# Alternating the two feed-forward products block by block, earlier gathers for the experts, and a semaphore clearing without its own barrier

## The reference, cut to what matters

```python
def _L0_ffn_ref(x, Wr, br, Wi, bi, Wg, bg, Wo, bo, gamma, beta):      # 8 experts, the best 2 of each token
    h = gelu(xf @ Wi_e + bi_e) * sigmoid(xf @ Wg_e + bg_e)
    r = xf + (h @ Wo_e + bo_e)                                        # then normalised, scaled and shifted
def _L1_ffn_ref(x, ln_gamma, ln_beta, fc1_q, fc1_scales, fc1_bias, fc2_q, fc2_scales, fc2_bias):
    h = (x - mu) * rsqrt(var + EPS) * ln_gamma + ln_beta
    y = silu(h.reshape(-1, H) @ dequant(fc1_q, fc1_scales) + fc1_bias)   # 256 -> 1024
    z = y @ dequant(fc2_q, fc2_scales) + fc2_bias                        # 1024 -> 256
    return x + 0.5 * z
x = _layernorm(x + _L0_attn_ref(...))       # a test-time-training layer
x = _layernorm(x + _L0_xattn_ref(...))
x = _layernorm(x + _L0_ffn_ref(...))        # mixture of experts
x = _layernorm(x + _L1_attn_ref(...))       # causal self-attention, 16 heads
x = _layernorm(x + _L1_xattn_ref(...))      # cross-attention over 1601 keys
x = _layernorm(x + _L1_ffn_ref(...))
```

## Time and profile before

| | |
|---|---|
| Median of 3 timed runs | 1908.94 us (1908.84 to 1918.33) |
| The profiled execution's own time | 1901.39 us |
| Its span | 1899.6 us, 33937 instructions |
| PE busy | 1710.2 us, 90% |
| DVE, ACT, POOL busy | 1366.7, 1041.8, 672.3 us |
| Expert stage, first to last PE product | about 405 to 756 us |
| Self-attention ends, cross-attention stage begins | 1054.3, 1059.9 us |
| Last stage | 1772.7 us to the end |

### The profile page before, as it was taken

One profiled execution on the slowest core, in us unless ns is written; L12 is line 12 of the kernel. 1 busy time (PEld: TensorE's weight loads), 2 busy tenths in 40 slices (PEclk: granted clock), 3 DMA queues, 4 the chain that ended last, 5 costly groups with the idle time before them and its releaser, 6 DMA issues. The chain is left out here.

```text
span 1899.6 us, 33937 instructions
## 1 busy us (share of the span) xinstructions
PE 1710.2 (90%) x13150; PEld 937.8 (49%) x13150; DVE 1366.7 (72%) x2346; ACT 1041.8 (55%) x1743; POOL 672.3 (35%) x754
## 2 busy tenths in 40 slices
PE   8999899989999997889999788599999999999786
PEld 4788577758888886423333555122222222223354
DVE  1534688756666666767775578989999999995663
ACT  1221555535555554336667243178888888886442
POOL 0555877124444442323320234313322121102452
PEclk9999999989999999969999899589999999999998
DMA  5134899866777673621110476321201011100001
GB/s 196 35 118 150 301 318 319 293 256 262 296 276 284 260 281 137 183 83 32 33 30 10 144 198 208 88 62 41 81 19 36 18 27 28 24 14 1 26 12 33
DMA packets 114083, 247.58 MB, mean 130 GB/s; under 512 B 28234, under 2 KB 83054, under 8 KB 110320
## 3 DMA queue, kind: packets, MB, share of 16 engines
q1 hardware_dynamic: 87636, 208.21, 31.6%
q0 software_dynamic: 24176, 35.12, 6.9%
q10 hardware_dynamic: 2112, 2.10, 0.3%
HBM read 183.39 MB, written 61.38 MB: 129 GB/s over the span
## 5 line engine op out<-in xcount | busy, mean ns | idle before, releaser
L2114 DVE TENSOR_REDUCE Eh_maxima<-Eh_max 128x2 f32<-128x802 f32 x512 | 474.7, 987 | 20.4 <-PE Eh_max L1993 15.3
L2102 ACT ACTIVATE Eh_probs<-Eh_pair 128x1024 f32<-128x1024 f32 (+1 forms) x288 | 287.5, 998 | 112.5 <-PE Eh_pair L2032 112.4
L1993 PE MATMUL Eh_max<-Eh_KS,Eh_QS 49*128 49x401 f16 x1024 | 197.3, 357 | 45.7 <-DVE Eh_maxima L2114 41.7
L1453 PE MATMUL C_y<-C_x_high,C_W 128*128 128x256 f16 (+1 forms) x1536 | 216.3, 254 | 8.9 <-ACT C_gate L1513 7.4
L2055 PE MATMUL Eh_av_ps<-Eh_probs,E_V 128*17 128x512 f32 (+1 forms) x1664 | 222.1, 606 | 0.0
L2114 DVE TENSOR_REDUCE Dh_maxima<-Dh_max 128x2 f32<-128x1024 f32 x128 | 152.1, 1222 | 43.9 <-PE Dh_max L2001 42.0
L1453 PE MATMUL C_y<-C_x_low,C_W 128*128 128x256 f16 (+1 forms) x768 | 181.3, 254 | 0.0
L2102 ACT ACTIVATE Eh_probs<-Eh_single 128x512 f32<-128x512 f32 x272 | 161.7, 595 | 26.8 <-PE Eh_single L2032 26.6
L1993 PEld LDWEIGHTS Eh_max<-Eh_KS,Eh_QS 49*128 49x128 f16 x1024 | 50.3, 94 | 234.2 <-DVE Eh_maxima L2114 199.2
L1831 POOL DMA_DIRECT2D Eh_KS<-E_kd x64 | 37.2, 581 | 352.7 <-PE Eh_pair L2032 347.9
L1453 PEld LDWEIGHTS C_y<-C_x_high,C_W 128*128 128x128 f16 x1536 | 139.5, 98 | 22.6 <-ACT C_gate L1513 9.6
(11 more groups left out here) (433 smaller groups left out, 3549.0 us busy)
## 6 DMA issues: line engine op xcount, KB each, us to landing
C_W<-w_split SPq DMA_DIRECT2D x24, 3072.0 KB, 11.8
w_split<-B_w_parts SPq DMA_DIRECT2D x24, 768.0 KB, 8.4
Eh_KS<-E_kd POOLq DMA_DIRECT2D x64, 150.1 KB, 3.3
C_tail<-in_expert_tail_dram SPq DMA_DIRECT2D x24, 384.0 KB, 8.5
B_places<-in_w_experts_dram SPq DMA_DIRECT2D x10, 768.0 KB, 6.8
A_QT<-in_w_experts_dram SPq DMA_DIRECT2D x8, 768.0 KB, 5.0
w_split<-A_QT SPq DMA_DIRECT2D x8, 768.0 KB, 6.7
early_more<-in_w_experts_dram SPq DMA_DIRECT2D x8, 768.0 KB, 10.0
```

Of the source, the lines that this page charges most:

```text
L1453: last = mm(y_ps[n % Y_BANKS][:, i, 0:w], W[:, u, a, at_w:at_w + P], x[:, s % 2, k, 0:w], start=(q == 0), stop=(q == len(parts) - 1))
L1993: last = self.nc.tensor.matmul(bank[:, a, 0:self.cw], self.QS[r, slot, p, qt * P:(qt + 1) * P], self.KS[r, slot, p, k0:k0 + self.cw], star ...
L2102: self.nc.scalar.activation(dst, src, ACT.Exp, scale=1.0 / SCORE).then_inc(self.exp_done, 1)
L2114: self.nc.vector.tensor_reduce(self.maxima[:, g % 2, :, p * TPB + qt, c], self.max_ps[n % 2][:, :, 0:self.cw], AX_X, ALU.max).then_inc(sel ...
```

## The change

In the expert stage a tile's gather moves from the tail of POOL's loop to its head. The barrier with clearing between self-attention and cross-attention goes; the attention blocks clear, on POOL, those ids that earlier stages have given back. `held.close()` gives the expert stage's semaphores back before the heads of self-attention. The last stage's biases are loaded in the cross-attention stage, where ACT also runs one sigmoid at its end, and the four normalisations of batch 1 move from there into the last stage. In the last stage the second product of block n-2 follows the first product of block n, for all four token tiles at once, each in its own PSUM bank; the hidden halves live in a ring of 8. DVE's and POOL's insertions are placed anew, and the last batch is stored in two parts.

```diff
@@ phase_moe, POOL
             for s in range(TILES):
+                if s + 3 < TILES:
+                    gather(s + 3)
                 if s + 1 < TILES:
                     base(s + 1)
                 for q in range(SIZES[s]):
                     finish(s, q)
                     scatter(s, q)
-                if s + 3 < TILES:
-                    gather(s + 3)
@@ LastStart
+        sp.dma_start(self.b1[:], self.dram["L1_ffn_fc1_bias"]).then_inc(self.small_loaded, 16)
+        sp.dma_start(self.b2[:], self.dram["L1_ffn_fc2_bias"].partition_broadcast(P)).then_inc(self.small_loaded, 16)
+
+    def warm_up(self, act):
+        act.wait_ge(self.scale_loaded, 32)
+        self.nc.scalar.activation(self.warm[:], self.gamma[:], ACT.Sigmoid).then_inc(self.warmed, 1)
...
                 v.tensor_copy(self.HT_parts[:, 0, 0], self.HT[:, 0]).then_inc(self.ht_high, 1)
-                self.normed_again(dve, 1)
@@
+def spent_semaphores(nc):
+
+    free = set(nc.free_semaphores)
+    return runs_of([s for s in nc.released_uncleared_semaphores if s in free])
...
@@ run_heads, and likewise phase_cross1 ahead of start.pool(pool)
+            for first, end in spent:
+                pool.sem_clear(range(first, end))
@@ phase_cross1
                 heads.scalar(act)
+                start.warm_up(act)
@@ phase_last
+    turn_ps = after.turn_ps = [ps(f"turn{h}", [P, S])[:] for h in range(KD)]
+    after.out_ps = [bank.rearrange("p (q d) -> p q d", d=D) for bank in turn_ps]
     y1_ps = [ps(f"y1_{i}", [P, S]) for i in range(2)]
-    y2_ps = [ps(f"y2_{i}", [P, D]) for i in range(2)]
+    y2_ps = [ps(f"y2_{t}", [P, S]) for t in range(TPB)]
@@ phase_last, SP
-            sp.dma_start(b1[:], dram["L1_ffn_fc1_bias"]).then_inc(small_loaded, 16)
-            sp.dma_start(b2[:], dram["L1_ffn_fc2_bias"].partition_broadcast(P)).then_inc(small_loaded, 16)
...
+            for first, end in STORES:
+                sp.wait_ge(norm_out.normed, end)
+                sp.dma_start(out[first * P:end * P, :].rearrange("(t p) d -> p t d", p=P), X[:, first:end, :]).then_inc(stored, 16)
@@ phase_last, PE
+            def narrow(n):
+                c, j = divmod(n, NF)
+                pe.wait_ge(hidden_low, n + 1)
+                for t in range(TPB):
+                    if j == 0 and c >= 1:
+                        pe.wait_ge(sum_ready, (c - 1) * TPB + t + 1)
                     for i, (a, x) in enumerate(((0, 0), (0, 1), (1, 0))):
-                        last = mm(y2_ps[n % 2][:], hidden_parts[:, c % 2, a, j, t * P:(t + 1) * P], w2_parts[:, x, j, :],
+                        last = mm(y2_ps[t][:, 0:D], hidden_parts[:, a, n % RING, t * P:(t + 1) * P], w2_parts[:, x, j, :],
                                   start=(j == 0 and i == 0), stop=(j == NF - 1 and i == 2))
+                    if j == NF - 1 and t < TPB - 1:
+                        last.then_inc(y2_ready, 1)
+                last.then_inc(narrowed, 1)
+
+            widen(0, 0)
             after.attended(pe, B - 1)
+            widen(0, 1)
+            for n in range(2, B * NF):
+                widen(*divmod(n, NF))
+                if n == 2:
+                    pe.wait_ge(after.copied, KD * B)
+                    turn(1)
+                    pe.wait_ge(w_loaded, 16)
+                if n == 5:
+                    pe.wait_ge(copied, 2 * KD)
+                    after.project(pe, B - 1)
+                if n == NF + 2:
+                    pe.wait_ge(after.sum_ready, NT // 2)
+                    turn(2)
+                if n == 2 * NF + 2:
+                    turn(3)
+                if n < B * NF - 1:
+                    narrow(n - 2)
+            for n in range(B * NF - 3, B * NF):
+                narrow(n)
@@ phase_last, POOL
-            for n in range(1, B * NF):
+            for n in range(B * NF):
                 low(n)
+                if n == 2:
+                    start.low(pool, 1)
+                if n == 4:
+                    norm_in.inverse_deviation(pool, 2)
+                if n == NF:
                     after.norm.inverse_deviation(pool, 3)
+                if n == NF + 3:
+                    start.low(pool, 2)
                 if n == NF + 4:
                     norm_in.inverse_deviation(pool, 3)
+                if n == 2 * NF + 3:
+                    start.low(pool, 3)
+                if n in (NF + 4, 2 * NF + 4, 3 * NF + 4):
+                    norm_out.inverse_deviation(pool, n // NF - 1)
...
@@ phase_last, DVE, from block 4 on
+            for n in range(4, B * NF):
+                c, j = divmod(n, NF)
+                step(n)
+                if n == 5:
+                    start.normed_again(dve, 2)
+                if n == 6:
+                    after.add(dve, 3)
+                    after.norm.statistics(dve, 3, after.sum_ready, per=2)
+                if n == NF:
+                    base(1)
+                if c >= 1 and j == 1:
+                    dve.wait_ge(base_ready, c)
+                    for t in range(TPB):
+                        add((c - 1) * TPB + t)
+                if n == NF + 2:
+                    start.again(dve, 3)
+                if c >= 1 and j == 3:
+                    norm_out.statistics(dve, c - 1, sum_ready)
+                if n == NF + 5:
+                    start.normed_again(dve, 3)
+                if n == NF + 6:
+                    base(2)
+                if n == 2 * NF:
+                    base(3)
+                if c >= 1 and j == 5:
+                    dve.wait_ge(norm_out.rstd_ready, c)
+                    normalize((c - 1) * TPB, c * TPB)
+            dve.wait_ge(base_ready, B)
+            for n in range(NT - TPB, NT):
+                add(n)
+                norm_out.statistics_of(dve, n, sum_ready)
@@ build_program
-                    phase_self(nc, own, dram, X, XT, ident, attended, carried, self_loaded)
+                    phase_self(nc, own, held, dram, X, XT, ident, attended, carried, self_loaded)
             routed.close()
-            renew_semaphores(nc)
```

More of the change, by code:

```diff
@@ L2982, in phase_cross1 @@
         start.use_banks(heads.max_ps)
+        spent = spent_semaphores(nc)
         with nc.Block(no_gpsimd_drain=True) as block:
@@ L3022, in phase_cross1 @@
     return start
+RING = 8
+STORES = [(c * TPB, (c + 1) * TPB) for c in range(B - 1)] + [(NT - TPB, NT - 1), (NT - 1, NT)]
 def phase_last(nc, ctx, dram, X, XT, ident, ATT, weight_parts, out, start):
@@ L3095, in _ @@
[L3095 to L3098, removed]
-            after.attended(pe, B - 1)
[L3100 to L3103, removed]
-                for j in range(NF):
-                    widen(c, j)
-                    narrow(c - 1, j // 2, range(NF // 2) if j % 2 == 0 else range(NF // 2, NF))
-                    if (c, j) == (1, 1):
-                        after.project(pe, B - 1)
-                    if (c, j) == (1, 5):
-                        turn(2)
-                    if (c, j) == (2, 5):
-                        turn(3)
@@ L3134, in high @@
             def high(n):
-                c, j = divmod(n, NF)
                 act.wait_ge(hidden_ready, n + 1)
-                if j == 0 and c >= 2:
-                    act.wait_ge(y2_ready, (c - 1) * TPB)
-                nc.scalar.copy(hidden_parts[:, c % 2, 0, j, :], hidden[:, n % 4, :]).then_inc(hidden_high, 1)
+                if n >= RING:
+                    act.wait_ge(narrowed, n - RING + 1)
+                nc.scalar.copy(hidden_parts[:, 0, n % RING, :], hidden[:, n % 4, :]).then_inc(hidden_high, 1)
             def step(n):
@@ L3201, in add, with normalize @@
             def add(n):
-                dve.wait_ge(y2_ready, n + 1)
-                v.scalar_tensor_tensor(X[:, n, :], y2_ps[n % 2][:], 0.5, X[:, n, :], ALU.mult, ALU.add).then_inc(sum_ready, 1)
+                c, t = divmod(n, TPB)
+                if t < TPB - 1:
+                    dve.wait_ge(y2_ready, c * (TPB - 1) + t + 1)
+                else:
+                    dve.wait_ge(narrowed, (c + 1) * NF)
+                v.scalar_tensor_tensor(X[:, n, :], y2_ps[t][:, 0:D], 0.5, X[:, n, :], ALU.mult, ALU.add).then_inc(sum_ready, 1)
+            def normalize(first, end):
+                for n in range(first, end):
+                    norm_out.normalize_of(dve, n)
             dve.wait_ge(small_loaded, 32)
@@ L3207, in _ @@
             step(0)
-            start.again(dve, 2)
+            start.normed_again(dve, 1)
             step(1)
+            after.norm.normalize(dve, 2)
             step(2)
+            norm_in.statistics(dve, 2, after.norm.normed)
+            step(3)
             dve.wait_ge(half_b2, 1)
             base(0)
-            for j in range(3, NF):
-                step(j)
-            for c in range(1, B):
-                for j in range(NF):
-                    step(c * NF + j)
-                    if (c, j) == (1, 0):
-                        start.normed_again(dve, 2)
-                    if (c, j) == (1, 1):
-                        after.add(dve, 3)
```

(20 more changed lines are left out.)

71 lines of the change are left out of this document (26 added, 45 removed).

## The result

The changed kernel takes 1862.54 us (median of 4, 1862.25 to 1863.48) against 1908.89 in the same session: a ratio of 0.9758 (0.9733 to 0.9782). Nine executions of it in two sessions have a median of 1865.5, 32 of the kernel before 1908.8. The forecast, 1874, was 8 to 12 us too high; the time lies at the low end of the range. The profiled execution took 1862.25 us (span 1860.4), 39.2 less in span than the one before, where I had summed 35.1.

A forecast was written before the change was run, and what follows sets the result against it. Expert and feed-forward stages were taken as PE-bound with holes. Gains 16.5 + 5.3 + 0.5 + 1.8 + 10.6 + 0.4 = 35.1 us give 1866.3 from the profiled 1901.39, 1873.8 from the timed 1908.94; forecast 1874, range 1862 to 1886.

The forecast's parts named there:

- Gathers, 16.5: Expert stage: gathers issued one tile sooner remove PE's eight waits, 16.5 of 17.0 us gained, bounds 10 and 17.5.
- rival B: Expert stage: PE waits for weights or biases instead, 1.5 us at each of eight places, 12 in all: 1886 us; chance 0.07.
- Border, 5.3: Between self-attention and cross-attention: dropping the barrier with its clearing gains 5.3 us, POOL's clears being hidden; bounds 3 to 5.6.
- rival D: Attention stages: POOL's clears do not overlap and hold a stage's end, the border's 5.3 us comes back: 1879 us; chance 0.06.
- Clock behind the border, 0.5: Start of cross-attention: PE may keep 2.4 GHz behind the short border, 0.5 us gained, bounds 0 and 3.
- End of cross-attention, 1.8: Without four normalisations on DVE, ACT's copy of the last sums starts 1.8 us sooner, and the next border too; bounds 0 to 1.9.
- Feed-forward stage, 10.6: Last stage: new product order and earlier loads take it from 114.0 to 103.4 us, 10.6 less; bounds 2 and 20.
- rival C: Last stage: PE's many short waits drop it to 1.2 GHz and keep it there, 90 us more: 1964 us; chance 0.03.
- Rival A: Feed-forward stage gains nothing: each block waits 0.35 us for its low half or hidden block, price 10.6: 1884.5 us; chance 0.10.
- Last store, 0.4 less: End of the kernel: the last store is 128 instead of 512 KB, 0.4 us gained, between 0 and 0.8.
- The sum: Whole kernel: all gains added, 35.1 us less than the profiled execution or the timed median.

The follow-up runs named there:

- the seventh: The changed kernel with an empty block at the third border, in which POOL clears the whole range of ids without a drain of POOL: 1866.3 us.
- the ninth run: The changed kernel once more, unchanged: median 1866.12 us, ratio 0.9781 to the kernel before.
- The border experiment: The kernel before with only the third border changed (no barrier, clears on POOL inside the attention stages): 1901.86 us, ratio 0.9965.

## Why the prediction was right, and where not

*Gathers, 16.5:* right, with all eight waits gone; weights and biases did not become late (rival B). Against the mean of the four old profiles it is 19.3, since the profiled one was short in this stage. That is above my bound of 17.5: 1.0 of it is clock, and some 1.3 are not in the list of waits.

*Border, 5.3:* right in size (6.4 to 1.1). The step that named the clearing as what costs was wrong; it was POOL's drain (3.98 us, against 0.78 for the clear). "No row shows a clear by itself" was wrong too: the view of line 3316 has both. That the clears hide (against rival D) held.

*Clock behind the border, 0.5:* the table has 3.4 for that stretch, the repeated change 0.3. That the border has a part in it is not shown: the stage's first 28 us had 3.5 to 6.1 us at the lower clock in the six profiles with the long border, and 0 (twice) to 6.2 in the other eight.

*End of cross-attention, 1.8:* right. With 57.4 us at the lower clock the heads take 573.8 before, 571.9 and 572.0 after (the seventh and the ninth run). The load starts 0.02 us behind the operation ahead of it, and its end and the next sigmoid are 0.01 us apart. The drain of 1.38 us that the Trainium skill, "ScalarE: Activation LUTs" ("What ACT_TABLE_LOAD costs"), adds to the load does not appear here, and the trace decides against it.

*Feed-forward stage, 10.6:* this term was mis-sized; it measured 15.0 (114.0 to 99.0, where I had named 100 to 107 as a sign). Two parts of the step failed. I took a slow start for certain (4.5 us with the filling); in the first trace the clock stayed at 2.4 GHz, and PE's idle times just before had become 0.81 and 1.15 instead of 2.65 and 1.30. These do not settle it: in four of the ten profiles with the changed stage it started at 1.2 GHz behind the same two, for 3.4 us. And I counted 8.3 us of waits behind it; the trace has 6.2. The list of waits was right in kind, POOL's low halves. But the longest that I had in the middle was 1.4 us, where it is 1.1 (block 15), and the longest of all, 2.2 us for the very last low half, I had not seen. In the ten profiles with the new order, the stage less half its time at the lower clock is 98.6 to 98.7 in the seven with a lag of two: it is PE-bound, and only the clock moves it. What I missed is on the old side: old orders spent 10 to 23 us of the stage at the lower clock, new ones 0 to 6. In the four old profiles this time lies at the stage's start (3.3 to 5.5 us), around and behind the wait before the third product (3.4 to 10.3) and at seven of the eight batch borders with their 3.3 us of waiting (3.4 each). The border experiment's last stage shows it best, with the old order's start and its batch border:

```profile
1773.00:1793.00 20.00, 12.00 (x40) 6.25 (x41) 7.77 (x18) 8.27 (x12) 6.67 (x6) 0.67 0.17 60
...
1813.00:1833.00 20.00, 16.72 (x108) 10.71 (x106) 13.12 (x31) 8.75 (x14) 10.35 (x10) 0.91 0.00 1
```

Half of the mean difference (16.7 against 2.4 us) is 7 us. The holes of 3 to 5 us thus seem to cost twice, as idle time and as half speed after; no run removed one of them alone at a fixed clock.

So rival C had the sign wrong. PE's short waits in the middle of the stage (up to 1.1 us, with a lag of three one of 2.3) did not lower the clock, and with the long ones gone it was higher than before. The one of 2.2 us at the end is less harmless: in four of the seven profiles with a lag of two the clock fell 1.2 to 1.3 us behind its end, here in the repetition, whose wait ends at 1856.60:

```profile
1765.00:1857.50 92.50, 86.39 (x585) 57.16 (x584) 57.86 (x125) 44.06 (x71) 51.27 (x47) 1.00 0.06 18
1858.00:1861.00 3.00, 2.79 (x14) 1.67 (x11) 1.88 (x7) 0.00 (x0) 0.00 (x0) 0.50 0.00 0
```

The rule of the Trainium skill, "TensorE: Matmul & The Clock Gate" ("A second HAM failure mode: psum-queue depth-cycling"), did not show here: the products alternate between banks all along, and from 4 us behind the stage's start to that last wait PEclk is 1.00 in each of the ten profiles. Rival A (1884.5) fell with the 15.0.

*Last store, 0.4 less:* wrong, it is 0.9 more in this pair: from the end of DVE's normalisations (and 1851.47 in the row below) to the span's end 8.9 against 8.1 us. From PE's last matmul it is 13.3 to 14.1 in the seven profiles with the changed last stage and a lag of two, 13.2 in the four with the old one.

```profile
1850.09 1.38 DVE L94 TENSOR_SCALAR X<-X,F_out_mv,F_out_rstd 128x256 f32<-128x256 f32 x4 [0.26 <-POOL F_out_rstd L82]
```

What failed is the path: the span does not end with the store. In the kernel before, SP's wait for the last store is over at 1894.5, and POOL's drain at the end of the block runs on to 1899.35; in the changed kernel these are 1854.1 and 1860.21. The views of the blocks' lines, before and after:

```profile
L3049 POOLq DRAIN  x1: 10284/10284/10284, 1889.1 to 1889.1; - x1
L3049 SPq COMPARE_BRANCH  x1: 41/41/41, 1894.5 to 1894.5; - x1
```

```profile
L3080 POOLq DRAIN  x1: 9837/9837/9837, 1850.4 to 1850.4; - x1
L3080 SPq COMPARE_BRANCH  x1: 41/41/41, 1854.1 to 1854.1; - x1
```

The drain ends 9.2 us behind POOL's last operation in both (and in the other twelve profiles), and in this pair that operation ends 4.3 instead of 3.4 us behind PE's last matmul, since it now waits for the last tile's statistics: that is the 0.9. (Where the last products ran at half clock, in four of the seven, it is 3.4 in the new order too.) So a smaller last store can gain nothing here, and the changed kernel still ends with some 6 us of POOL's drain alone. No run took it out.

*The sum:* 35.1. At the same mean granted clock, 0.955, lines through the 32 and the 9 executions give 1904.0 and 1869.0, a difference of 35.0. That it is so near is luck in part. With half the time at the lower clock taken off, the feed-forward stage gains 7.5 (106.2 on the mean of three old profiles against 98.7) where I had 10.6, the experts 18.3 where I had 16.5, and the last store has the wrong sign; the errors offset each other. The further 8 us of the medians go with the clock: the change's executions had 0.957 on average and the others 0.952, which no term of mine foresaw. The range held the result by luck as well: the larger gains named for its low end add up to 42.0, which from 1908.94 is 1867 and not 1862.

## What to carry to other kernels

A hole of some us in a PE-bound stage can cost more than its length, because the clock may come back late (2.74 instead of 1.46 us for the product behind 3.29 us of waiting); price it from both rows, the wait and the product behind it. Before comparing two single traces, set each stage's length beside its time at the lower clock: here stages that nobody touched differed by up to 6 us. And before a barrier is built away, ask which of its parts is late: the view of its line lists them, and drained beside other work the same barrier cost 1.4 instead of 5.5 us. At the end of a kernel ask the same: here the last store is not what it ends with.

## What the hardware showed unexpectedly

- A drain of POOL, idle for over 50 us, took 4.0 to 4.1 us at the border, and at the end of the last stage it ended 9.2 us behind POOL's last operation. A second drain with nothing in between took 0.11 us, clearing the whole range of semaphores 0.78.
- The clock granted behind one and the same pair of idle times (1.59 and 1.15 us) was 1.00 in two profiles and 0.50 to 0.53 in four; behind 0.81 and 1.15 us it was 1.00 in six and 0.50 in four. What decides it isn't settled: the rows just ahead of it are the same.
- A lower clock in one stage is not a property of the code alone: self-attention, the same code in all fourteen profiles but for POOL's clears and drain, had 40 to 57 us of it and took 293.5 to 300.0 us.
